# Norms made inside the end of the stage ahead of them, and a softmax split between two engines

## The reference, cut to what matters

```python
x = x + L0_xattn(ctx, norm(x))        # time warping path between ctx and x
x = x + L0_ffn(norm(x))               # ternary weights, conv, 8-bit activations
x = x + L1_xattn(ctx, norm(x), ctx)   # 8 heads, two softmaxes per head
x = x + L1_ffn(norm(x))               # 8 experts, the best 2 for each token
x = x + L2_xattn(norm(x), ctx, ctx, mask)   # 16 heads of 8
x = x + L2_ffn(norm(x))               # soft mixture of 64 experts, 32 slots each
x = x + L3_xattn(norm(x), ctx, ctx)   # 16 heads of 8, with biases
x = x + L3_ffn(norm(x))               # 6 experts, chosen by a 6-bit code tanh(z / 0.3)
```

## Time and profile before

| what | us |
|---|---|
| median of 3 runs (lowest, highest) | 1143.43 (1139.03, 1148.41) |
| profiled execution, its own time | 1140.56 |
| its span, first to last instruction | 1138.76, printed as 1138.8 |
| busy: TensorE, VectorE | 883.1, 797.6 |
| busy: ScalarE, GpSimd | 547.1, 450.1 |
| mean granted TensorE clock, share of full | 0.894 |

### The profile page before, as it was taken

How to read it: one execution, slowest core, us unless ns; L and a number is a source line. 1 busy time by engine, 2 the same in 40 slices (tenths; PEclk the granted TensorE clock), 3 DMA queues, 4 the chain that set the end, 5 groups by cost and what they waited for, 6 DMA issues and landing times. The chain is left out here.

```text
span 1138.8 us, 25983 instructions
## 1 busy us (share of the span) xinstructions
PE 883.1 (78%) x10221; PEld 630.8 (55%) x10221; DVE 797.6 (70%) x1848; ACT 547.1 (48%) x1106; POOL 450.1 (40%) x282
## 2 busy tenths in 40 slices
PE   4173597699649992699666998989898897668977
PEld 3062353587526762245444766767676676525556
DVE  4988686688464545588576869587786957669754
ACT  3061244355424444356475474664747463236554
POOL 4000220586227773686005333352633333269500
PEclk9587699899759996799788999999999999879979
DMA  4311001200051122000100000000000000000001
GB/s 142 100 55 75 1 1 37 118 2 2 28 195 47 52 52 88 1 2 1 47 0 2 25 3 24 3 24 26 3 25 2 25 3 3 2 1 1 1 1 38
DMA packets 27053, 35.80 MB, mean 31 GB/s; under 512 B 7825, under 2 KB 20372, under 8 KB 26166
## 3 DMA queue, kind: packets, MB, share of 16 engines
q1 hardware_dynamic: 21238, 27.71, 7.5%
q0 software_dynamic: 2496, 5.12, 1.7%
q10 hardware_dynamic: 3200, 1.31, 0.4%
HBM read 26.85 MB, written 7.27 MB: 30 GB/s over the span
## 5 line engine op out<-in xcount | busy, mean ns | idle before, releaser
L1741 POOL TENSOR_TENSOR soft_spread<-soft_spread,soft_inv 128x1024 f32<-128x1024 f32 x31 | 81.1, 2645 | 188.7 <-DVE soft_inv L1822 133.9
L1602 PE MATMUL soft_expert_ps<-soft_W,soft_slots 128*32 128x128 f32 x4096 | 137.9, 277 | 14.7 <-issue 8.6
L1829 DVE TENSOR_TENSOR soft_outs<-soft_expert_ps,soft_bias 128x512 f32<-128x512 f32 x128 | 87.4, 688 | 82.8 <-PE soft_expert_ps L1602 82.8
L1602 PEld LDWEIGHTS soft_expert_ps<-soft_W,soft_slots 128*32 128x32 f32 x4096 | 106.2, 110 | 47.3 <-issue 43.7
L1682 ACT ACTIVATE soft_slots<-soft_slot_ps 128x512 f32<-128x512 f32 x128 | 69.4, 593 | 84.7 <-PE soft_slot_ps L1588 82.9
L796 POOL TENSOR_TENSOR l_prob<-l_prob,l_inv 128x1024 f32<-128x1024 f32 x48 | 91.3, 1901 | 41.3 <-DVE l_inv L907 41.3
L1736 POOL TENSOR_TENSOR soft_spread<-soft_spread,soft_peak 128x1024 f32<-128x1024 f32 x28 | 66.4, 2371 | 76.0 <-ACT soft_comb L1691 76.0
L890 DVE TENSOR_REDUCE l_top<-l_score 128x16 f32<-128x1024 f32 x48 | 58.5, 1218 | 34.3 <-PE l_score L966 13.0
L187 PE MATMUL ln_turned<-ident,xn_tok 128*128 128x128 f32 x112 | 30.1, 437 | 65.6 <-DVE xn_tok L116 65.6
L1588 PE MATMUL soft_slot_ps<-soft_spread,xn_tok 64*128 64x256 f32 x512 | 75.4, 415 | 1.2 <-DVE soft_spread L1794 1.2
L1691 ACT ACTIVATE soft_comb<-soft_spread,soft_neg 128x256 f32<-128x256 f32 x128 | 63.3, 501 | 27.2 <-DVE soft_neg L1774 24.9
(11 more groups left out here) (343 smaller groups left out, 2074.0 us busy)
## 6 DMA issues: line engine op xcount, KB each, us to landing
moe_w<-in_moe_W SPq DMA_DIRECT2D x2, 2048.0 KB, 9.9
soft_W<-in_soft_W SPq DMA_DIRECT2D x16, 256.0 KB, 2.7
kept<-early SPq DMA_DIRECT2D x1, 2048.0 KB, 6.2
l_keys<-in_moe_b SPq DMA_DIRECT2D x1, 2048.0 KB, 8.6
l_asked<-kept SPq DMA_DIRECT2D x1, 2048.0 KB, 12.9
ctxT<-in_ctxT SPq DMA_DIRECT2D x1, 1024.0 KB, 5.5
moe_rows<-xn_tok SPq DMA_DIRECT2D x4, 256.0 KB, 3.6
l_values<-moe_back SPq DMA_DIRECT2D x4, 256.0 KB, 4.9
```

The lines of the kernel that those rows point to most:

```text
L1602: last = nc.tensor.matmul(expert_ps[c][32 * j:32 * j + 32, h, tt, :], slots[u % 3][:, h, tt, 128 * c + 32 * j:128 * c + 32 * j + 32], W[i ...
L1741: nc.gpsimd.tensor_tensor(spread[j % 2][:, quarter(k), :], spread[j % 2][:, quarter(k), :], wide(inv), ALU.mult).then_inc(share_done, 1)
L1829: nc.vector.tensor_tensor(outs[u % 3][:, c].rearrange("p h t d -> p (h t) d"), expert_ps[c][:].rearrange("p h t d -> p (h t) d"), bias[i % ...
```

## The change

`layernorm` as a block is gone (but for the first norm, `first_norm`). A class `Norm` holds its pieces (`statistics`, `variances`, `normalise`, `take_v`, `deviate`, `shift_rows`, `take_a`, `turn`), and each stage's engines call them between the instructions of their last iterations, or behind them. In `attend`:

```diff
 VectorE, at the end of iteration i, ahead of add(i - 5), T = 16:
+                if i == T:
+                    dve.wait_ge(added, 8)
+                    for t in range(8):
+                        norm.statistics(t)
+                    norm.variances(dve, 0)
+                    norm.variances(dve, 1)
+                if i == T + 1:
+                    dve.wait_ge(added, 12)
+                    for t in range(8, 12):
+                        norm.statistics(t)
+                    norm.variances(dve, 2)
+                    norm.normalise(dve, 0)
+                if i == T + 2:
+                    norm.normalise(dve, 1)
+                if i == T + 3:
+                    norm.normalise(dve, 2)
+                if i == T + 4:
+                    dve.wait_ge(added, 15)
+                    for t in range(12, 15):
+                        norm.statistics(t)
 TensorE:
+                if i == T + 2:
+                    pe.wait_ge(prob_done, T)
+                    norm.turn(pe, 0)
+                if i == T + 3:
+                    norm.turn(pe, 1)
+            norm.turn(pe, 2)
+            for g in range(G):
+                if g == 2:
+                    norm.turn(pe, 3)
+                if read:
+                    norm.ready(pe, g)
+                    read(pe, g, mix).then_inc(read_done, 1)
 ScalarE, behind the evictions of iteration i:
+                if i == T:
+                    norm.begin()
+                    norm.deviate(act, 0)
+                    norm.deviate(act, 1)
+                if i == T + 1:
+                    norm.deviate(act, 2)
+                    norm.shift_rows(act, 0)
+                if i == T + 2:
+                    norm.shift_rows(act, 1)
+                    norm.take_a(act, 0)
+                if i == T + 3:
+                    norm.shift_rows(act, 2)
+                    norm.take_a(act, 1)
+            norm.deviate(act, 3)
+            norm.shift_rows(act, 3)
```

The bit feed-forward makes ln2 and l1's queries in its end (`ask`), the experts ln4 and l2's queries, the soft experts ln6 and l3's queries; each has the same calls placed by hand. In the bit feed-forward, as in `attend`, statistics of tiles 0 to 7 stand ahead of add 13, transposes of group 0 ahead of `lower_tile(15)`. At the end of the experts:

```diff
 GpSimd, behind the last scatter:
+            pool.wait_ge(raised_done, TILES)
+            for r in range(RING):
+                pool.wait_ge(scattered[r], 16 * len(range(r, TILES, RING)))
+            queries.lay_apart(pool)
+            pool.wait_ge(x_done, G)
+            for t in range(4):
+                queries.spread(t)
 VectorE, in the loop over g that adds the returned rows to x:
+                dve.wait_ge(x_done, g + 1)
+                for t in range(4 * g, 4 * g + 4):
+                    norm.statistics(t)
+                norm.variances(dve, g)
+                if g:
+                    norm.normalise(dve, g - 1)
+            norm.normalise(dve, G - 1)
+            norm.take_v(dve, 2)
+            norm.take_v(dve, 3)
+            queries.take_v(dve, 1)
+            queries.take_v(dve, 3)
```

The softmax of `attend` is split, KEEP = 12:

```diff
-                nc.scalar.activation(prob[...], shifted[t % 2][...], ACT.Exp, scale=exp_scale).then_inc(prob_done, 1)
+                nc.scalar.activation(by_score[:, 0:KEEP // sets], shifted[t % 2][...], ACT.Exp)
+                for n in range(KEEP, 16):
+                    last = nc.scalar.activation(by_score[:, n // sets, n % sets, :], scores[t % 2][:, n, :], ACT.Exp,
+                                                bias=under[t % 2][:, n:n + 1])
+                last.then_inc(prob_done, 1)
-                nc.vector.tensor_tensor(shifted[t % 2][:], scores[t % 2][:], top[...], ALU.subtract)
+                nc.vector.tensor_tensor(shifted[t % 2][:], scores[t % 2][:, 0:KEEP, :], under[...], ALU.add)
```

More of the change, by code:

```diff
@@ L170, in _ @@
[L170 to L178 removed]
+                    norm.shift_rows(act, g - 1)
@@ L190, in _ @@
-            if after:
-                for g in range(G):
-                    pe.wait_ge(xnT_a if g < G // 2 else xnT_v, g % 2 + 1)
-                    after(pe, g)
-    core.wait_x = core.wait_consts = False
+            pe.wait_ge(core.loaded["consts"], core.consts_count)
+            for g in range(G):
+                norm.turn(pe, g)
 def warp(nc, core):
@@ L352, in _ @@
             pe.wait_ge(sums_done, 2)
-            nc.tensor.matmul(total[:], core.ones[:], sums[:], start=True, stop=True).then_inc(total_done, 1)
+            nc.tensor.matmul(total, core.ones[:], sums[:], start=True, stop=True).then_inc(total_done, 1)
             pe.wait_ge(core.loaded["taps"], 16)
@@ L616, in lower_tile, with ask @@
                 last.then_inc(down_done, 1)
+            def ask(g):
+                norm.ready(pe, g)
+                for q in range(4):
+                    last = nc.tensor.matmul(norm.banks[g][:, 128 * q:128 * q + 128], core.l1_xq[:, q, 8 * g:8 * g + 8, :],
+                                            core.l1["Wq"][:], start=True, stop=True)
+                last.then_inc(asked_done, 1)
             turn_in(0)
@@ L1250, in _, with weigh @@
             bring_back(act, 0)
+            norm.begin()
             act.wait_ge(shares_done, 1)
-            for g in range(G):
+            def weigh(g):
                 act.wait_ge(back_in[0][g], 16)
@@ new lines, in _, with head_attention, score, output @@
+            norm.take_v(dve, 3)
+            queries.take_v(dve, 1)
+            queries.take_v(dve, 3)
+def head_attention(nc, core, name, w, masked, queries, next_norm, **read):
+    qT, values = queries.qT, queries.values.rearrange("p (t m w) -> p t m w", t=T, m=8)
+    def score(out, keys, t):
+        keys = keys.rearrange("p (a b s) -> p a b s", a=8, b=2)
+        for r in range(2):
+            rows = slice(64 * r, 64 * r + 64)
+            for b in range(2):
+                own = qT[rows, 128 * t + 64 * b:128 * t + 64 * b + 64]
+                last = nc.tensor.matmul(out[64 * b:64 * b + 64, 8 * r:8 * r + 8, :], own, keys[rows, :, b, :],
+                                        start=True, stop=not masked)
+        if masked:
+            hidden = core.mask_bias[:, S * t:S * t + S].unsqueeze(1).broadcast_to([128, 8, S])
+            for r in range(2):
+                last = nc.tensor.matmul(out[:, 8 * r:8 * r + 8, :], core.ident16[:], hidden, start=False, stop=True)
+        return last
+    def output(out, mixedT):
+        for i in range(2):
+            for b in range(2):
+                nc.tensor.matmul(out[64 * b:64 * b + 64, 0:128], mixedT[:, i, 64 * b:64 * b + 64], w["Wo"][:, b, i, :],
+                                 start=(i == 0), stop=False)
+        return nc.tensor.matmul(out[:, 0:128], core.ones16[:], core.bias16[:, 1 if masked else 2, :], start=False, stop=True)
+    attend(nc, core, name, score, lambda t, m: values[:, t, m], output, 1.0,
+           lambda out, t: spread_heads(nc, core, queries.kT, out, t), queries.ring, 4, next_norm, **read)
@@ L1751, in _ @@
                     share(j, k)
+            pool.wait_ge(core.kept_in, 16)
+            pool.wait_ge(turn_done, 8 * I)
+            queries.lay_apart(pool)
+            for t in range(4):
+                queries.spread(t)
         @block.vector
@@ L1914, in _ @@
                         put(g - 3)
+                    if not ahead and g in (4, 6):
+                        survey_rows(range(2 * g - 8, 2 * g - 4))
+                        norm.variances(dve, g // 2 - 2)
+                    if not ahead and g in (5, 7):
+                        norm.normalise(dve, g // 2 - 2)
                     if ahead and g >= 4:
```

847 lines of the change are left out of this document (464 added, 383 removed).

## The result

The changed kernel takes 1107.12 us (median of 4 runs, 1104.57 to 1113.65) against 1144.07 (1139.03 to 1148.41): ratio 0.9683, 95% interval 0.9652 to 0.9714, some 36 us less. The profiled execution took 1105.92 us, its span is 1104.1. The forecast was 1112, with a range of 1098 to 1129.

A forecast was written before the change was run, and what follows sets the result against it. No engine is near full; stages with different limits meet at six serial seams, together 104 us. Terms -1.7 - 6.0 + 1.5 - 4.0 - 9.0 - 8.0 - 4.0 = -31.2 give 1109.4 profiled, median 1112, range 1098 to 1129.

The forecast's parts named there:

- rival A: Holds and clock turn out kind: GpSimd misses VectorE, TensorE stays at 2.4 GHz through the reads; 9 better, 1103; chance 0.22.
- The tails: Ends of all three attentions: norm pieces go into VectorE's idle time, the first ahead of add 11; last add 1.9 us later.
- l2 to soft: Seam from l2 attention to the soft experts: 7.0 us instead of 11.0, -4.0.
- l1 to routing: Seam from l1 attention to expert routing: 8.0 or 12.1 us by TensorE's clock against 16.6; middle less mask conversion, -6.0.
- l3 to codes: Seam from l3 attention to the codes, up to first scaling: 16.7 to 20.7 us against 26.7, -8.0.
- bit to l1: Seam from bit feed-forward to l1 attention: last add later, yet first score at about 211.3 against 213.0, -1.7.
- soft to l3: Seam from soft experts to l3 attention: 9 to 11.5 us to the first score against 20.2, 1 subtracted for holds, -9.0.
- experts to l2: Seam from experts to l2 attention: GpSimd's copies and spreads hold VectorE; first score 470.2 against 468.7, +1.5; without holds -3.
- The loops: Attention loops: shift covers 12 of 16 heads, ScalarE takes four by small Exps; -2 l1, -2 l2, -1 l3, +1 last sums, -4.0.
- B: Tails pull the clock down: TensorE waits between short bursts, reads and query matmuls slower; 16 worse, 1128; chance 0.22.
- C: Small Exps cost 0.49 us each, lengthening all three attention loops: 1153; decides from 0.43 us each; chance 0.03.
- D: In-order queues give back in tails what seams save, last adds 5 us late in each of six: 1133; chance 0.08.

The follow-up runs named there:

- e7_norm_at_end: Changed kernel with the whole norm of the three attentions behind the last add, still in the attention's own block: 1127.0 us, ratio 0.9844.
- e0_changed: The changed kernel unaltered, run again to compare other runs with it, and a second profile of it: 1110.14 us, ratio 0.9692.
- e4_lay_in_block: Changed kernel with GpSimd's clearing, copies and first spreads for l2 and l3 back at the start of the attentions' own blocks: 1118.39 us, ratio 0.9768.
- e2_holds: Changed kernel with GpSimd's bias split, first spread ahead of l1 and four spreads at the experts' end made to wait, out of VectorE's way: ratio 0.9696.
- e11_warm: As e7_norm_at_end, plus 40 TensorE transposes of the identity into a free bank while it waits for the first normalised rows: ratio 0.9808.

## Why the prediction was right, and where its steps were off

The sum was -31.2, the profiles show -34.7; the median came out 5 us under the forecast, between it and rival A (1103). That the sum is so near is in part luck: the rows of the table miss by 8.5 us upwards and by 11.9 downwards. The cause, waiting at the seams that goes when the norm stands in the stage ahead, is the one forecast, and the experiments show it. One reading of the seams before was too broad: "every engine is busy for half of the window or a little more" does not hold for GpSimd (0 to 9.6 us) nor for TensorE from l2 to the soft experts (4.28 of 11.0). Point by point:

*The tails.* "The last add comes 1.9 us later": measured 2.28 and 2.26 in l1 and l2, and 0.6 sooner in l3. TensorE's wait of 2.31 us behind add 11 is the one named, but the number was right by luck, for it is a sum of three. The pieces of norm cost 1.8 us (10.04 at a clock of 1.00, 8.25 in e7_norm_at_end without them). Against the kernel before, the tail had become 0.9 shorter (9.14 to 8.25), for which the shorter bias matmul (0.48 to 0.23 us a tile) is the likely reason, not tried alone; the prediction gave it nothing here. And 1.4 us are the clock, 0.85 in these tails and 1.00 in those before; in l3 it was the other way round.

*l2 to soft, l1 to routing* (-3.5 and -6.4 for -4.0 and -6.0): near. In l1 the second read took 3.14 us at 1.2 GHz, the first 1.85 at 2.4, so the middle of both that was chosen was the truth. The mask's conversion cost more than the 0.5 forecast: beside GpSimd's two instructions for it VectorE's first TENSOR_SCALAR of the routing took 0.99 us (0.23 in the kernel before) and its first TENSOR_TENSOR 0.84 (0.29), 1.3 in all.

*l3 to codes* (-11.9 for -8.0): the mis-sized term is the clock. Of the 3.9 us, 2.5 lie in the tail (+1.9 forecast, -0.6 measured, clock 0.85 before and 1.00 after), and the rest where the middle of 5.4 and 9.5 us was taken and the reads ran at 2.4 GHz throughout. It is a draw of this profile: in e0_changed the stretch is 28.41 us, 9.0 less than before.

*bit to l1* (-5.8 for -1.7): two terms. The last add was put 5.8 to 6.2 us late and is 3.4 late (behind warp's last x): ScalarE's table load had begun before VectorE's statistics were done and was not added to them. And the 32 query matmuls met a clock of 0.92, not the 0.64 of before.

*soft to l3* (-12.0 for -9.0): first score 8.2 us behind the last x where 9 to 11.5 had been counted, clock 1.00 (9.48 us at 0.82 in e0_changed), and none of the 1 us of holds, as GpSimd had long finished. e4_lay_in_block shows that 9.7 of 12.0 are GpSimd's laying ahead, the term that the prediction mentioned as fitting in and didn't name as the main gain.

*experts to l2* (+3.2 for +1.5): the holds were sized well. The adds beside the copies lost 2.3 us (2.4 forecast); the last x came 8.0 us later behind the last scatter (8.2 forecast); the last normalisation ended 29.8 us behind the last scatter, forecast 465 - 434.9 = 30.1. But the step from there was wrong: not the queries release the next block but GpSimd, 7.7 us behind its last spread. The price of the spreads is thus not the 5 us by which they hold VectorE, which are hidden behind that wait. e2_holds took the hold away and lost 2.9 us.

The rule of the Trainium skill, page SBUF — State Buffer, section "Who interferes with whom", is borne out by what VectorE's two-input instructions show (0.28 to 0.94 us). The pair of normalisations that grew from 0.60 to 3.85 us are TENSOR_SCALARs with one wide SBUF input; the same section lists `tensor_scalar` among the operations that can enter a two-port mode and then contend with GpSimd too. These rows agree with that, though no run here shows in which mode they ran.

*The first stage* (+3.1 for 0): this step failed outright. "The bias split in the first stage hides under the VectorE-only path search; uncovered it would cost 5": VectorE alone was taken for cover, while its instructions there have two SBUF inputs and GpSimd's six CASTs and TENSOR_TENSORs hold them, the very mechanism that the prediction used two stages on. e2_holds gave 2.6 us of it back by one wait.

*The loops* (-4.5 for -4.0; 2.8 in the profile of e0_changed): shift 0.27 shorter, small Exps 0.229 apart, forecast 0.27 and 0.24; maxima 4.17, 4.05 and 3.82 us apart, forecast 4.24, 4.04 and 3.9. The period of l3, which was said to be at the limit of shift, Exp and sum, is at GpSimd's 2 x 1.90 instead.

*Rivals.* B (tails pull the clock down) came true in the tails of l1 and l2, 1.4 us each where it had 1, and in the second read of l1; for the seams as a whole it was wrong in direction, for their clocks rose from between 0.53 and 0.66 to between 0.69 and 1.00. C's price was 0.43 us an Exp, measured 0.229. D's last adds 5 us late in each of six are 2.3 late in l1 and l2, 3.4 in the bit stage and 8.0 in the experts, and earlier in l3.

## What to carry to other kernels

Work that a seam repeats for all tiles belongs into the idle time of the stage ahead, but behind the instruction that another engine waits for, not ahead of it: the order of one add and one piece of norm was worth more than the softmax split. Ask of each moved instruction not only whether the engine is idle there but what it holds elsewhere, GpSimd beside VectorE above all; and where a block ends, ask which engine's last instruction releases the next one, since removing a stall ahead of another engine's end gained nothing here. A ratio over the whole kernel (here good to 3 us) can't see a gain of 2.5; the periods and marks of the trace can. But read the granted clock of a stretch beside its length: the same tail took 10.0 us at 1.00 and 11.4 at 0.85, and a mark read from one profile has that coin toss in it.

## What the hardware showed that was not expected

- Behind the experts' block the next one starts 7.7 us behind GpSimd's last instruction in each of eight profiles with four spreads there, while VectorE had ended 1.4 to 8.0 us ahead of that start; with one late spread it is 8.0. In the bit and soft experts' blocks the next first score comes 1.24 and 1.33 us behind GpSimd. GpSimd had issued 78 indirect DMAs in the former and none in the latter two. The cause is open.
- Six GpSimd instructions of 0.5 to 0.9 us each beside VectorE's chain of small two-input instructions lengthened that by 2.6 to 3.1 us.
- In e11_warm TensorE had a granted clock of 1.00 while it was busy 2.77 of 3.95 us, and of 0.50 in the 4.60 us that followed a read of 1.85 us without a wait: 16 small matmuls took 1.86 us and the next 16 3.42. The clock fell while TensorE was at work, behind waits of under 1 us, although 40 matmuls had just kept it busy.
